# Eight PSUM banks for the transposed tiles of two norms, and the third norm's statistics split around the last residual additions

## The chip, the cores and the metric

The kernel runs on one core of a Trainium2 chip. The metric is the device time of one execution in microseconds (us); the median of three runs of the kernel before is 2484.04 us. A core has TensorE (PE, with its weight loads as PEld), VectorE (DVE), ScalarE (ACT), GpSimd (POOL) and SyncE (SP), which here only issues DMAs. PSUM, into which PE writes, has eight banks of 512 f32 columns over 128 partitions; the kernel names them `bank[:, 0..7, :]`.

## The reference, cut to what matters

One decoder layer on x of shape (2, 512, 512): two batches of 512 tokens with 512 features, so 1024 tokens in eight tiles of 128 (tiles 0 to 3 are the first batch, 4 to 7 the second). Three layer norms stand ahead of the causal attention, the group (self and cross) attention and the experts:

```python
x = x + attn(layernorm(x), ...)            # first norm, causal attention with 16 heads
x = x + xattn(layernorm(x), ctx_2048, ...) # second norm, 8 groups, self and cross attention, fp8 rounding
x = x + ffn(layernorm(x), ...)             # third norm, router, 8 experts with silu gate

def _layernorm(x, axis=-1, eps=1e-05):
    m = jnp.mean(x, axis=axis, keepdims=True)
    v = jnp.var(x, axis=axis, keepdims=True)
    return (x - m) / jnp.sqrt(v + eps)
```

## The kernel before, in words

The layer is written as blocks that follow each other: `first_norm`, `causal_attention`, `second_norm`, `group_attention`, `experts`. Each block holds one program for each engine, and all engines meet at its end before the next block begins; within a block only semaphores order them.

The residual stream is `X` in SBUF, eight tiles of 128 tokens x 512 f32. A norm has two halves.

**Statistics**, on DVE alone. `tile_stats` (L251) takes one `bn_stats` over a tile. `finish_stats` takes four `bn_aggr` (L259) and then a reciprocal square root in twelve tiny steps (L57 to L63), each waiting for the one before, and a shift (L263), which raises `s_shift`. It does so for the four tiles of a batch at once. `norm_stats` runs both over all eight tiles: four `bn_stats`, finish batch 0, four `bn_stats`, finish batch 1.

**Apply, turn, split**, in `norm_scalar` (ACT), `norm_tensor` (PE) and `norm_lo` (DVE). For each batch, ACT first writes four normalised tiles `xn` (L279), and then, for each of them, waits until PE has transposed it (four 128x128 f32 transposes into one bank, L293, `s_turned`) and copies the bank to the f16 high part `XTh` (L283, `s_hi`). DVE subtracts that from the bank, which gives the f16 low part `XTl` (L270, `s_lo`). ACT turns to the next batch's `xn` only behind the last `XTh` of this one. PE writes tile t into bank `t % 2`, and so before tile t it waits until the low part of tile t - 2 is done.

The first norm runs at the start of the kernel: `X` arrives by eight DMAs, then the weights of the first head quad. Its DVE program is `norm_stats`, then `w.split_lo` (L158, which needs the high part from POOL, L154), then `norm_lo`. The second norm (L1047, L1205) has code of its own and doesn't call the three functions; its statistics (after the causal attention) are already written as batch 0, additions, batch 1.

The third norm's statistics stand at the end of `group_attention`. There the last group's output is rounded to fp8 (`output_round` on DVE, `quantised` on POOL, L1485, into `cat`), PE runs four output jobs Y0 to Y3 for the second batch (eight matmuls each, L1781 and L1782, in two banks by turns, so that Y2 waits until Y0's sum has been added), and DVE adds each to `X` (`project_out`, L1657, semaphore `y_added`). `norm_stats` for `rows3` comes behind all four additions. The first batch's additions were done a step earlier.

`experts` begins with the third norm's apply, turn, split (`norm_scalar`, `norm_tensor`, `norm_lo`, on `eXTh` and `eXTl`). Beside it, SP issues the router's weights and the first expert's `raw_gate`, `raw_up`, `raw_down` (2 MB each). POOL writes the f16 high parts of gate and up (four pieces each, L1919), as they land. DVE goes on behind `norm_lo` with the router's low part `rwl` (L1978), and then the low parts of gate and up, four pieces each (`split_lo`, L1973). PE runs the router (96 small matmuls, behind `rwl` and the last low part), then the experts: for each of 16 blocks twelve gate matmuls and twelve up matmuls; the first gate matmul of an expert waits for all four low pieces of gate, the first up matmul for all four of up. From then on PE is never short of work for long.

The two functions that the changed lines call directly:

```python
def tile_stats(dve, n, src, t):
    dve.bn_stats(n.stats[:, t, :], src[:, t, :]).then_inc(n.s_stats, 1)
def finish_stats(dve, n, b, use=0):
    tiles = slice(BT * b, BT * (b + 1))
    for t in range(BT * b, BT * (b + 1)):
        dve.wait_ge(n.s_stats, NT * use + t + 1)
        dve.bn_aggr(n.mv[:, t, :], n.stats[:, t, :]).then_inc(n.s_mv, 1)
    dve.wait_ge(n.s_mv, NT * use + BT * (b + 1))
    rsqrt(dve, n.s_rsqrt, RSQRT_STEPS * (B * use + b), n.mv[:, tiles, 1], n.half[:, tiles], n.rstd[:, tiles],
          n.tmp[:, tiles])
```

Of the kernel before, what the change touches and what calls it, by code (L numbers as in the profile page):

```python
# [24 lines left out]
P = 128  # L25
# [3 lines left out]
BT = S // P  # L29
KT = D // P  # L30
# [16 lines left out]
def rsqrt(dve, sem, base, var, half, out, tmp):  # L47

    k = 0

    def step(ins):
        nonlocal k
        ins.then_inc(sem, 1)
        k += 1
        dve.wait_ge(sem, base + k)

    step(dve.tensor_scalar(half, var, EPS, None, ALU.add))  # L57
    step(dve.tensor_scalar(tmp.bitcast(I32), half.bitcast(I32), 1, None, ALU.arith_shift_right))
    step(dve.tensor_scalar(out.bitcast(I32), tmp.bitcast(I32), -1.0, RSQRT_SEED, ALU.mult, ALU.add))
    for _ in range(NEWTON):  # L60
        step(dve.tensor_tensor(tmp, out, out, ALU.mult))
        step(dve.scalar_tensor_tensor(out=tmp, in0=tmp, scalar=-0.5, in1=half, op0=ALU.mult, op1=ALU.mult))
        step(dve.scalar_tensor_tensor(out=out, in0=tmp, scalar=1.5, in1=out, op0=ALU.add, op1=ALU.mult))  # L63
    assert k == RSQRT_STEPS


def after(eng, sem, count):

    if not isinstance(count, int) or count > 0:
        eng.wait_ge(sem, count)  # L70
# [100 lines left out]
def first_norm(nc, ins, sem, sb, bank, X, ident, cols, XTh, XTl, x_d, w):  # L171
# [7 lines left out]
    with nc.Block() as block:  # L179
# [17 lines left out]
        @block.vector  # L197
        def _(dve):
            norm_stats(dve, rows, X, lambda t: dve.wait_ge(x_in[t], 16))
            w.split_lo(dve, 0)  # L200
            norm_lo(dve, tiles, XTh, XTl, bank)

        @block.scalar
        def _(act):
            norm_scalar(act, tiles, X, XTh, bank)

        @block.tensor
        def _(pe):
            pe.wait_ge(id_set, 2)
            norm_tensor(pe, tiles, bank, ident)  # L210
# [30 lines left out]
def norm_stats(dve, n, src, arrived, use=0):  # L241

    for t in range(NT):
        arrived(t)
        tile_stats(dve, n, src, t)
        if (t + 1) % BT == 0:
            finish_stats(dve, n, t // BT, use)
# [15 lines that stand above are left out]
    dve.scalar_tensor_tensor(out=n.shift[:, tiles], in0=n.mv[:, tiles, 0], scalar=-1.0, in1=n.rstd[:, tiles],  # L263
                             op0=ALU.mult, op1=ALU.mult).then_inc(n.s_shift, 1)


def norm_lo(dve, n, XTh, XTl, bank):
    for t in range(NT):
        dve.wait_ge(n.s_hi, t + 1)
        dve.tensor_tensor(XTl[:, :, t * P:(t + 1) * P], bank[:, t % 2, :].rearrange("p (k c) -> p k c", k=KT),  # L270
                          XTh[:, :, t * P:(t + 1) * P], ALU.subtract).then_inc(n.s_lo, 1)


def norm_scalar(act, n, X, XTh, bank):
    for b in range(B):
        tiles = range(BT * b, BT * (b + 1))
        act.wait_ge(n.s_shift, b + 1)
        for t in tiles:
            act.activation(n.xn[:, t, :], X[:, t, :], ACT.Identity, scale=n.rstd[:, t:t + 1],  # L279
                           bias=n.shift[:, t:t + 1]).then_inc(n.s_xn, 1)  # L280
        for t in tiles:
            act.wait_ge(n.s_turned, t + 1)
            act.activation(XTh[:, :, t * P:(t + 1) * P], bank[:, t % 2, :].rearrange("p (k c) -> p k c", k=KT),  # L283
                           ACT.Copy).then_inc(n.s_hi, 1)


def norm_tensor(pe, n, bank, ident):
    for t in range(NT):
        pe.wait_ge(n.s_xn, t + 1)
        if t >= 2:  # L290
            pe.wait_ge(n.s_lo, t - 1)
        for k in range(KT):
            ins = pe.transpose(bank[:, t % 2, k * P:(k + 1) * P], n.xn[:, t, k * P:(k + 1) * P], ident[:])  # L293
        ins.then_inc(n.s_turned, 1)


# [551 lines left out]
def round_fp8(dve, sem, base, y, unit, total):  # L848

    dve.tensor_scalar(y, y, FP8_MAX, -FP8_MAX, ALU.min, ALU.max).then_inc(sem, 1)
    dve.wait_ge(sem, base + 1)
    dve.tensor_scalar(unit.bitcast(U16), y.bitcast(U16), 0x7F80, 0x40, ALU.bitwise_and, ALU.bitwise_or).then_inc(sem, 1)
    dve.wait_ge(sem, base + 2)
    dve.tensor_scalar(unit, unit, 1.5 * 2.0 ** -6, 2.0 ** 4, ALU.max, ALU.mult).then_inc(sem, 1)
    dve.wait_ge(sem, base + 3)
    dve.tensor_tensor(total, y, unit, ALU.add).then_inc(sem, 1)
# [470 lines left out]
def group_attention(nc, ins, sem, sb, bank, X, ident, cols, rcols, xq, kv_d, gw, rows3, qr, v0):  # L1329
# [6 lines left out]
    STEPS = GROUPS * B  # L1336
# [29 lines left out]
    next_done, next_read, y_done, y_added = (sem(f"x_{x}") for x in ("next_done", "next_read", "y_done", "y_added"))  # L1366
# [39 lines left out]
    with nc.Block() as block:  # L1406
# [229 lines left out]
        def _(dve):  # L1636
# [17 lines left out]
            def project_out(n, t, b):  # L1654
                dve.wait_ge(y_done, y_count(t, n))
                x = X[:, BT * b + t, :]
                dve.scalar_tensor_tensor(out=x, in0=JOB[job_bank(f"Y{t}", n + 2)], scalar=psc[:], in1=x, op0=ALU.mult,  # L1657
                                         op1=ALU.add).then_inc(y_added, 1)
# [20 lines left out]
            def output_round(n, kind):  # L1679
                count = KINDS * n + kind  # L1680
                dve.wait_ge(o_read, count + 1)
                after(dve, rounded, count)
                round_fp8(dve, rounding, ROUND_STEPS * count, y[:], unit[:], total[:])
# [44 lines left out]
            parts_lo(STEPS - 1, UX - 1)  # L1728
            for kind in range(1, KINDS):
                output_round(STEPS - 1, kind)  # L1730
            for t in range(BT):
                project_out(STEPS - 1, t, 1)

            norm_stats(dve, rows3, X, lambda t: dve.wait_ge(y_added, BT * (STEPS - 1) + max(0, t - BT + 1)))

        @block.tensor
        def _(pe):
# [118 lines left out]
def experts(nc, ins, sem, sb, bank, X, ident, out_d, rows3):  # L1856
# [38 lines left out]
    with nc.Block() as block:  # L1895
# [39 lines left out]
        def _(act):  # L1935
            def split_hi(e, i, k):
# [3 lines left out]
                act.activation(piece(wh, i, k), piece(raw, i, k), ACT.Copy, scale=WS).then_inc(w_hi[i], 1)  # L1940

            norm_scalar(act, n, X, XTh, bank)
            act.wait_ge(rw_in, 16)
            act.activation(rwh[:], rw[:], ACT.Copy, scale=WS).then_inc(rw_hi, 1)
# [25 lines left out]
        def _(dve):  # L1970
            def split_lo(e, i, k):
                dve.wait_ge(w_hi[i], PW * e + k + 1)
                dve.scalar_tensor_tensor(out=piece(wl, i, k), in0=piece(raw, i, k), scalar=WS, in1=piece(wh, i, k),  # L1973
                                         op0=ALU.mult, op1=ALU.subtract).then_inc(w_lo[i], 1)

            norm_lo(dve, n, XTh, XTl, bank)
            dve.wait_ge(rw_hi, 1)
            dve.scalar_tensor_tensor(out=rwl[:], in0=rw[:], scalar=WS, in1=rwh[:], op0=ALU.mult, op1=ALU.subtract)\  # L1978
# [70 lines left out]
        @block.tensor  # L2049
        def _(pe):  # L2050
            norm_tensor(pe, n, bank, ident)
            pe.wait_ge(rw_lo, 1)
            pe.wait_ge(n.s_lo, NT)
# [98 lines left out]
```

## Time and profile before

| what | us |
|---|---|
| median of three runs (2480.91 to 2487.3) | 2484.04 |
| profiled execution, its own time | 2486.31 |
| its span, from the first to the last instruction | 2484.5 |
| PE busy | 2317.3 |
| DVE busy | 1415.6 |
| ACT busy | 1138.5 |
| POOL busy | 1152.1 |

The profiled execution's time is 1.8 us more than its span. Times in the profile count from the first instruction. The first norm lies at 0 to 28 us, the third norm's statistics at 1452 to 1463 us, its apply, turn and split at 1463 to 1477 us, and the experts from there to the end. "Granted clock" is the share of TensorE's full clock: 1.00 is 2.4 GHz and 0.50 is 1.2 GHz.

### The profile page before, as it was taken

What the parts mean: (1) busy time and instruction counts of PE and PEld (TensorE: products, weight loads), DVE (VectorE), ACT (ScalarE), POOL (GpSimd) and SP (SyncE); (2) the same over time, 40 slices, a digit from 0 to 9 for tenths busy, and PEclk for the clock granted to TensorE, in tenths of its full rate; (3) what the DMA queues carried; (4) which work ended last, traced back from release to release, by engine and by line L of the source; (5) the groups of instructions that cost most, each with busy time, mean ns of one, the idle gap of its engine ahead of it and who ended that gap; (6) DMA issues with size and microseconds to landing.
All of it is one profiled execution on the core that took longest, in us unless ns stands there. A gap on an engine that the chain in (4) does not pass through costs nothing. (4 is left out here: it accounts for less than half of the span.)

```text
span 2484.5 us, 39824 instructions
## 1 busy us (share of the span) xinstructions
PE 2317.3 (93%) x14528; PEld 1308.1 (53%) x14528; DVE 1415.6 (57%) x2936; ACT 1138.5 (46%) x2165; POOL 1152.1 (46%) x1396
## 2 busy tenths in 40 slices
PE   6899888968999999999999859999999999999999
PEld 3566544535666666666666534444444444444444
DVE  5766687437999989999999852222222222222221
ACT  3455465447777778877778721111111111111110
POOL 2422327656787878778786324131313131313131
PEclk9799799979999999999999969999999999999999
DMA  4100012127878888888888741101010101010000
GB/s 151 35 19 18 1 60 103 76 102 158 157 149 164 155 167 162 159 155 154 166 151 150 138 152 73 68 34 68 34 68 34 68 34 67 35 67 35 0 0 34
DMA packets 437986, 224.81 MB, mean 90 GB/s; under 512 B 406224, under 2 KB 410320, under 8 KB 433616
## 3 DMA queue, kind: packets, MB, share of 16 engines
q1 hardware_dynamic: 415952, 186.74, 33.0%
q10 hardware_dynamic: 21888, 36.19, 5.6%
q8 instruction: 84, 1.38, 0.2%
q14 instruction: 62, 0.51, 0.1%
HBM read 103.34 MB, written 18.87 MB: 49 GB/s over the span
## 5 line engine op out<-in xcount | busy, mean ns | idle before, releaser
L1955 ACT ACTIVATE sil<-bank 128x512 f32<-128x512 f32 x128 | 76.4, 597 | 772.4 <-PE bank L301 772.4
L1928 POOL TENSOR_SCALAR hh<-h 128x512 f16<-128x512 f32 x128 | 105.1, 821 | 679.4 <-DVE h L2026 679.4
L2026 DVE TENSOR_TENSOR h<-bank,sil 128x512 f32<-128x512 f32 x128 | 88.6, 692 | 530.6 <-PE bank L301 422.8
L1572 ACT ACTIVATE xprob<-bank,xnm 128x1024 f32<-128x1024 f32 (+1 forms) x240 | 220.2, 917 | 185.2 <-DVE xnm L1663 185.0
L1675 DVE SCALAR_TENSOR_TENSOR xparts<-xprob,xri,xparts 128x1024 f16<-128x1024 f32 (+1 forms) x240 | 273.2, 1138 | 3.3 <-ACT xparts L1580 3.2
L1663 DVE TENSOR_REDUCE xnm<-bank 128x1 f32<-128x512 f32 (+1 forms) x256 | 242.9, 949 | 50.7 <-PE bank L301 49.3
L1580 ACT ACTIVATE xparts<-xprob,xri 128x1024 f16<-128x1024 f32 (+1 forms) x240 | 227.7, 949 | 0.0
L299 PE MATMUL bank<-eXTh,ewh_gate 128*128 128x512 f16 x512 | 194.8, 380 | 3.5 <-DVE ewl_gate L1973 3.5
L300 PE MATMUL bank<-eXTh,ewl_gate 128*128 128x512 f16 x512 | 194.8, 380 | 0.0
L301 PE MATMUL bank<-eXTl,ewh_gate 128*128 128x512 f16 x512 | 194.7, 380 | 0.0
L299 PE MATMUL bank<-eXTh,ewh_up 128*128 128x512 f16 x512 | 194.1, 379 | 0.0
L300 PE MATMUL bank<-eXTh,ewl_up 128*128 128x512 f16 x512 | 194.0, 379 | 0.0
L301 PE MATMUL bank<-eXTl,ewh_up 128*128 128x512 f16 x512 | 194.0, 379 | 0.0
L299 PE MATMUL bank<-ewh_down,hh 128*128 128x512 f16 x512 | 194.0, 379 | 0.0
L300 PE MATMUL bank<-ewh_down,hl 128*128 128x512 f16 x512 | 194.0, 379 | 0.0
L301 PE MATMUL bank<-ewl_down,hh 128*128 128x512 f16 x512 | 194.0, 379 | 0.0
L2036 DVE SCALAR_TENSOR_TENSOR X<-bank,wcol,X 128x512 f32<-128x512 f32 x64 | 48.0, 751 | 214.9 <-PE bank L301 214.9
L1930 POOL TENSOR_TENSOR hl<-h,hh 128x512 f16<-128x512 f32 x128 | 153.3, 1198 | 22.6 <-POOL hh L1928 21.2
L299 PE MATMUL bank<-xpt,xkv 128*128 128x256 f16 x512 | 140.8, 275 | 8.9 <-DMA xpt<-xparts 8.8
L1470 POOL TENSOR_SCALAR qr<-qr,xrstd,xshift 128x128 f32<-128x128 f32 x240 | 147.4, 629 | 1.7
L300 PE MATMUL bank<-xpt,xkv 128*128 128x256 f16 x512 | 140.8, 275 | 0.0
L301 PE MATMUL bank<-xpt,xkv 128*128 128x256 f16 x512 | 140.7, 275 | 0.0
(289 smaller groups left out, 5966.7 us busy)
## 6 DMA issues: line engine op xcount, KB each, us to landing
xkv<-kv_made ACTq DMA_DIRECT2D x64, 256.0 KB, 3.3
raw_gate<-in_gate SPq DMA_DIRECT2D x8, 2048.0 KB, 7.8
raw_up<-in_up SPq DMA_DIRECT2D x8, 2048.0 KB, 7.9
raw_down<-in_down SPq DMA_DIRECT2D x8, 2048.0 KB, 7.8
xwraw<-in_w_group ACTq DMA_DIRECT2D x60, 256.0 KB, 3.4
kv_made<-vst SPq DMA_DIRECT2D x16, 512.0 KB, 4.2
kv_made<-kst SPq DMA_DIRECT2D x16, 512.0 KB, 2.6
kvraw<-in_w_kvx SPq DMA_DIRECT2D x4, 1024.0 KB, 6.7
```

The lines of the kernel that those rows point to most:

```text
L299: pe.matmul(ps, ah, bh, start=start, stop=False)
L300: pe.matmul(ps, al, bh, start=False, stop=False)
L301: return pe.matmul(ps, ah, bl, start=False, stop=stop)
L1470: pool.tensor_scalar(norm_block(i), norm_block(i), rstd[:, i:i + 1], shift[:, i:i + 1], ALU.mult, ALU.add)\
L1572: act.activation(prob[prob_of(u)][:, 0:L], SC[u % 2][:, 0:L], ACT.Exp, bias=nm[:, u % 4:u % 4 + 1], accum_out=rs[:, u % 4:u % 4 + 1]).then ...
L1580: act.activation(parts[u % PARTS_KEPT][:, 0:L], prob[prob_of(u)][:, 0:L], ACT.Copy, scale=ri[:, u % 4:u % 4 + 1]).then_inc(hi, 1)
L1663: dve.tensor_reduce(nm[:, s:s + 1], SC[u % 2][:, 0:L], AX.X, ALU.max, negate=True).then_inc(maxed, 1)
L1675: dve.scalar_tensor_tensor(out=part[:, L:2 * L], in0=prob[prob_of(u)][:, 0:L], scalar=ri[:, u % 4:u % 4 + 1], in1=part[:, 0:L], op0=ALU.mu ...
L1928: pool.tensor_scalar(hh[half][:, f, :], h[i % 2][:], 1.0, 1.0, ALU.mult, ALU.mult).then_inc(h_hi, 1)
L1930: pool.tensor_tensor(hl[half][:, f, :], h[i % 2][:], hh[half][:, f, :], ALU.subtract).then_inc(h_lo, 1)
L1955: act.activation(sil[i % 2][:], bank[:, 2 * (i % 2), :], ACT.Silu, scale=1.0 / WS).then_inc(silu, 1)
L2026: dve.tensor_tensor(h[i % 2][:], bank[:, 2 * (i % 2) + 1, :], sil[i % 2][:], ALU.mult).then_inc(made, 1)
```

## The change

In the first and the third norm, tile t is transposed into bank t instead of bank `t % 2`, and PE's wait for the low part of tile t - 2 is gone. At the end of `group_attention`, the first batch's third-norm statistics are issued on DVE ahead of the last four `project_out`, and only the second batch's behind them; the waits on `y_added` are placed accordingly.

```diff
 def norm_lo(dve, n, XTh, XTl, bank):
     for t in range(NT):
         dve.wait_ge(n.s_hi, t + 1)
-        dve.tensor_tensor(XTl[:, :, t * P:(t + 1) * P], bank[:, t % 2, :].rearrange("p (k c) -> p k c", k=KT),
+        dve.tensor_tensor(XTl[:, :, t * P:(t + 1) * P], bank[:, t, :].rearrange("p (k c) -> p k c", k=KT),
                           XTh[:, :, t * P:(t + 1) * P], ALU.subtract).then_inc(n.s_lo, 1)
...
         for t in tiles:
             act.wait_ge(n.s_turned, t + 1)
-            act.activation(XTh[:, :, t * P:(t + 1) * P], bank[:, t % 2, :].rearrange("p (k c) -> p k c", k=KT),
+            act.activation(XTh[:, :, t * P:(t + 1) * P], bank[:, t, :].rearrange("p (k c) -> p k c", k=KT),
                            ACT.Copy).then_inc(n.s_hi, 1)
 
 
 def norm_tensor(pe, n, bank, ident):
     for t in range(NT):
         pe.wait_ge(n.s_xn, t + 1)
-        if t >= 2:
-            pe.wait_ge(n.s_lo, t - 1)
         for k in range(KT):
-            ins = pe.transpose(bank[:, t % 2, k * P:(k + 1) * P], n.xn[:, t, k * P:(k + 1) * P], ident[:])
+            ins = pe.transpose(bank[:, t, k * P:(k + 1) * P], n.xn[:, t, k * P:(k + 1) * P], ident[:])
         ins.then_inc(n.s_turned, 1)
...
             for kind in range(1, KINDS):
                 output_round(STEPS - 1, kind)
+            dve.wait_ge(y_added, BT * (STEPS - 1))
+            for t in range(BT):
+                tile_stats(dve, rows3, X, t)
+            finish_stats(dve, rows3, 0)
             for t in range(BT):
                 project_out(STEPS - 1, t, 1)
-
-            norm_stats(dve, rows3, X, lambda t: dve.wait_ge(y_added, BT * (STEPS - 1) + max(0, t - BT + 1)))
+            for t in range(BT):
+                dve.wait_ge(y_added, BT * (STEPS - 1) + t + 1)
+                tile_stats(dve, rows3, X, BT + t)
+            finish_stats(dve, rows3, 1)
```

## Rows read from the trace of the kernel before

**Rows 1.** The page: busy time of each engine, and the chain that ended last, by line.
```profile
PE 2317.3 (93%) x14528; PEld 1308.1 (53%) x14528; DVE 1415.6 (57%) x2936; ACT 1138.5 (46%) x2165; POOL 1152.1 (46%) x1396
...
PE bank L299 13%; PE bank L300 13%; PE bank L301 13%; DVE ewl_gate L1973 0%; ACT xn_n L279 0%; PE bank L293 0%; ACT eXTh L283 0%; DVE eXTl L270 0%; DVE rwl L1978 0%; DVE X L2036 0%
```

**Rows 2.** The chain in order of time, third norm: start, us, what.
```profile
1463.06 2.93 ACT xn_n L279 x4
...
1476.68 0.69 DVE eXTl L270
1477.38 0.96 DVE rwl L1978
1478.33 6.23 DVE ewl_gate L1973 x4
```

**Rows 3.** Timeline, first norm: start, us, engine, line, operation [idle before, releaser].
```profile
10.23 2.93 ACT L279 ACTIVATE xn_n<-X,shift_n,rstd_n 128x512 f32<-128x512 f32 x4 [8.22 <-DVE shift_n L263]
...
11.19 1.94 PE L293 MATMUL bank<-ident,xn_n 128*128 128x128 f32 x8 [11.19 <-ACT xn_n L279]
...
13.07 1.06 ACT L283 ACTIVATE XTh<-bank 128x512 f16<-128x512 f32 x2
...
15.28 0.16 DVE L263 SCALAR_TENSOR_TENSOR shift_n<-mv_n,rstd_n 128x4 f32<-128x4 f32 x1
15.36 1.75 DVE L158 SCALAR_TENSOR_TENSOR wl<-wraw,wh 128x1536 f16<-128x1536 f32 x1
17.03 1.28 DVE L270 TENSOR_TENSOR XTl<-bank,XTh 128x512 f16<-128x512 f32 x2
...
17.86 1.94 PE L293 MATMUL bank<-ident,xn_n 128*128 128x128 f32 x8 [4.73 <-DVE XTl L270]
18.98 0.60 ACT L283 ACTIVATE XTh<-bank 128x512 f16<-128x512 f32 x1 [4.86 <-PE bank L293]
...
20.33 2.92 ACT L279 ACTIVATE xn_n<-X,shift_n,rstd_n 128x512 f32<-128x512 f32 x4
...
27.20 0.69 DVE L270 TENSOR_TENSOR XTl<-bank,XTh 128x512 f16<-128x512 f32 x1 [0.16 <-ACT XTh L283]
28.18 0.20 POOL L406 MEMSET identb<- 128x128 bf16 x1 [15.32 <-POOLq L179]
```

**Rows 4.** Timeline, end of the group attention, 1440 to 1458 us.
```profile
1440.45 1.15 POOL L1485 TENSOR_TENSOR cat<-xtotal,xunit 128x512 f16<-128x512 bf16 x1 [5.40 <-DVE xtotal L858]
...
1445.36 0.75 DVE L1657 SCALAR_TENSOR_TENSOR X<-bank,psc,X 128x512 f32<-128x512 f32 x1 [4.98 <-PE bank L1782]
...
1447.89 0.38 PE L1781 MATMUL bank<-xw3h,cat 128*128 128x512 f16 x1
...
1451.54 0.75 DVE L1657 SCALAR_TENSOR_TENSOR X<-bank,psc,X 128x512 f32<-128x512 f32 x1 [0.98 <-PE bank L1782]
1452.21 2.46 DVE L251 BATCH_NORM_STATS2 stats_n<-X 128x6 f32<-128x512 f32 x4
...
1457.45 2.46 DVE L251 BATCH_NORM_STATS2 stats_n<-X 128x6 f32<-128x512 f32 x4
```

**Rows 5.** Timeline, DVE, statistics of the second norm, near 307 us.
```profile
306.83 1.15 DVE L57 TENSOR_SCALAR half_n<-mv_n 128x4 f32<-128x4 f32 x1
```

**Rows 6.** Timeline, POOL, DVE and PE, first expert's weights; x1 rows are single pieces.
```profile
1471.34 4.07 POOL L1919 TENSOR_SCALAR ewh_gate<-raw_gate 128x1024 f16<-128x1024 f32 x4 [29.73 <-DMA raw_gate<-in_gate]
1476.24 6.11 POOL L1919 TENSOR_SCALAR ewh_up<-raw_up 128x1024 f16<-128x1024 f32 x4 [0.83 <-DMA raw_up<-in_up]
...
1479.39 2.05 DVE L1973 SCALAR_TENSOR_TENSOR ewl_gate<-raw_gate,ewh_gate 128x1024 f16<-128x1024 f32 x1
...
1484.48 4.62 DVE L1973 SCALAR_TENSOR_TENSOR ewl_up<-raw_up,ewh_up 128x1024 f16<-128x1024 f32 x4
...
1489.15 0.39 PE L299 MATMUL bank<-eXTh,ewh_up 128*128 128x512 f16 x1
```

**Rows 7.** Windows: busy us (instructions) of each engine, granted clock, DMA share, GB/s.
```profile
60.00:65.00 5.00, 5.00 (x43) 3.05 (x42) 2.76 (x6) 2.63 (x9) 5.00 (x11) 0.50 0.00 1
```

## The prediction

> **What bounds the kernel now.** I read the page's busy times and its chain first. PE is busy for 2317.3 us of 2484.5, and the chain that ended last consists of PE's matmuls but for a few small links of the third norm [rows 1]. So in most of the kernel an idle engine costs nothing, and only a stretch in which PE has no work can be shortened by this change. The busy share doesn't find such stretches; the chain in order of time and the timeline do. There are three:
>
> - 10 to 28 us. Nothing of the causal attention can begin before the first norm's block ends. The last instruction of that block is DVE's eighth low part at 27.20 us, and the next block's first instruction follows at 28.18 [rows 3].
> - 1452 to 1463 us. PE is out of work, and DVE takes the statistics of both batches, one behind the other [rows 4].
> - 1463 to 1489 us. The chain runs through the third norm's ACT, PE and DVE links, then the router's low part, then the four low pieces of gate [rows 2]; the low pieces of up end at 1484.48 + 4.62 = 1489.10, and the first up matmul starts at 1489.15 [rows 6]. What sets the experts' pace is therefore the end of up's low pieces, not the end of the norm.
>
> What comes behind each of these is relative to the block's start or to that up matmul, so a us taken off the last event of a stretch is a us off the end.
>
> **First norm, banks.** PE's wait before tile 2 is for tile 0's low part. DVE gives it only at about 17.7 us, since its batch-1 statistics (to 15.44) and the weight split of 1.75 us stand ahead of it. So PE idles 4.73 us, ACT waits 4.86 us for tile 2, and ACT's second batch starts at 20.33, though its shift was ready at 15.44 [rows 3]. Without the wait:
>
> - PE: eight transposes take 1.94 us with the last one's 0.42 in it, so they start 0.217 apart and a tile is 0.87. The tiles start at 11.19, 12.06, 12.93 and 13.80.
> - ACT: a high part started 18.98 - 17.86 = 1.12 us behind its tile's first transpose. Tile 2's starts at 14.05 and tile 3's at 14.92. ACT is free at 15.4, and the second batch's `xn` starts at about 15.5 instead of 20.33.
> - From `xn` to the first high part took 13.07 - 10.23 = 2.84, and to the first transpose 0.96. High parts 4 and 5 start at 18.3 and 18.8. The tiles 6 and 7 start at 18.2 and 19.1, their high parts at 19.3 and 20.2, and the last is done at 20.8.
> - DVE: it begins its low parts at 17.03 as now; two take 1.28, so a step is 0.60. Eight steps without a wait put the last start at 17.03 + 7 x 0.60 = 21.23, behind ACT's 20.8. So DVE is late last, not ACT or PE.
>
> The block's last instruction starts at 21.23 instead of 27.20: **-5.97 us**. Should each low part wait for a semaphore and take the whole 0.69 of a single one, it is 17.03 + 7 x 0.69 = 21.86, or -5.3. A faster PE clock would change nothing, as DVE sets the end. I take 5.97, since the pairs show 0.60. The weight DMA and POOL's split end before 15.36, as L158 needs them, and SP has nothing after them but the small `cols` load, so nothing else holds this block.
>
> **Third norm, statistics.** One batch takes 1457.45 - 1452.21 = 5.24 us on DVE [rows 4]. The first batch's moves ahead of the additions, into a hole: DVE finished its rounding just before POOL's `cat` at 1440.45 and idled 4.98 us until 1445.36 [rows 4]. Started at 1440.4, it ends at 1445.6, so the first addition is late by 0.3 us. What is queued behind it is Y0's addition, and Y2 on PE waits for that. Y2 starts at 1447.89 today, while the addition would end at 1445.6 + 0.75 = 1446.4. So there are 1.5 us of slack, and the chain Y0 to Y3 and the last addition at 1451.54 don't move. The second batch follows at 1452.21 as the first does now and ends 5.24 us sooner: **-5.24 us** for the block's end. The new waits on `y_added` hold nothing: the first batch's additions are a step old, and each of the second batch's is issued at least three `bn_stats` or additions ahead of the wait for it.
>
> Two neighbours need a price. `cat` runs beside the moved `bn_stats` and releases PE's Y0. If `bn_stats` held it up for its whole length, it would be at most 1.15 us, all of it on the path. In the first norm POOL's split ran beside four `bn_stats` and was in time for L158, and ACT's and DVE's rows there show no delay, so I take 0. The other is DVE's own L57. In the second norm's statistics, which already have this form, it took 1.15 us instead of 0.17 beside a POOL `tensor_tensor` [rows 5]. Here `cat` ends at 1441.6 and L57 comes at about 1440.4 + 2.4 + 0.4 = 1443.2, so they don't meet; if they did, 1.0 us would still fit in the 1.5 of slack. Cost 0.
>
> The Trainium skill says the same of such a pair: "SBUF — State Buffer", section "Who interferes with whom", lets a DVE `tensor_scalar` in a two-port mode take a port that it shares with GpSimd and wait for GpSimd's whole instruction. By that rule alone the move could cost DVE up to one `cat`; the sum would stay the same by it, because of the slack.
>
> **Third norm, banks.** Count from ACT's first `xn`, at 1463.06 [rows 2]. Today the last low part starts at 13.62 there. By the steps above: tile 3 starts at 0.96 + 2.61 = 3.57, its high part at 4.69, the second `xn` at 5.15, tile 7 at 8.72, its high part at 9.84, and its low part at 10.5. That is 3.1 us sooner, and it would be the whole gain if DVE could go on at the same pace. It can't. DVE's next work, `rwl` and eight low pieces, has two SBUF inputs, and POOL's high pieces run at the same time. A high piece alone takes 4.07 / 4 = 1.02 us, but the four of up take 6.11; a low piece alone takes 4.62 / 4 = 1.15, but 2.05 where POOL is at work, and `rwl`, a 128x32 tile, needs 0.96 [rows 2, 6]. They take turns. From 1478.33 to 1489.10 the pair did eight low pieces and two of up's high pieces in 10.8 us, so a high piece in turn adds 10.8 - 8 x 1.14 = 1.7 for two, or 0.84 each.
>
> POOL's pieces don't move: gate's data land at 1471.34 and up's at 1476.24, 8.28 and 13.18 by this count [rows 6]. DVE comes to `rwl` at 11.1, in the third of gate's high pieces, and gets its turn at 11.3. Then every turn is taken: eight low pieces at 1.14, and five high pieces (gate's last and all four of up, where today only two are left) at 0.84. 11.3 + 0.1 + 9.1 + 4.2 = 24.7, against 26.04 today. So up's low pieces end **1.3 us** sooner, and I take 1.2, as the other order (POOL's last gate piece first, at 1.0) gives 1.1. The low bound is POOL's and DVE's whole work back to back from 8.28: 8 x 1.02 + 0.1 + 8 x 1.14 = 17.4, or 25.7 against 26.04: 0.4. The high bound is 3.1.
>
> Gate's matmuls start some 2 to 3 us sooner, at 18.4 to 19.6, but they wait for up's weights again afterwards: twelve of them at half clock (0.43 each) take 5.1 us and end before 24.7. So that start is worth nothing, and the stall moves from ahead of gate to between gate and up.
>
> **Sum.** 5.97 + 5.24 + 1.2 = 12.4 us. From the profiled execution's own time, 2486.31, that gives 2473.9 (the 1.8 us around the span stay). It was 2.3 us over the median of the runs; against 2484.04 the time is **2471.6 us**, 0.50% less.
>
> **Rivals.**
>
> - *The whole 3.1 us of the third norm come through,* since POOL, waiting, falls behind without holding DVE. For it: `rwl` and the next low piece ran in one go. Against it: single low pieces at 2.05 [rows 6]. 14.3 us, 2469.7. Chance 0.1.
> - *The first norm's gain does not reach the end,* because the causal attention's start is held by something that doesn't move with the block. All I see there is relative (1 us from the block's start at 28.18). Then 6.4 us are left, 2477.6, which is within 0.3% (7.5 us; that is about what a measurement of this kernel tells from no change). Chance 0.07.
> - *The clock falls in the new gap between gate and up,* so that up's first matmuls run at 1.2 GHz. Some eight of them at 0.43 instead of 0.22 is 1.7 us; the gap is about 1 us. 10.7 us, 2473.3. This is inside the first case's range. Chance 0.12.
> - *Slower: the causal attention runs longer at half clock.* There PE is full and yet the granted clock is 0.50 at times, as at 60 to 65 us [rows 7]. Starting 6 us earlier could shift those stretches. Each us more of full PE work at half clock costs 0.5 us. To end 7.5 us above today it needs 20 us of loss, or 40 us more of half clock; half of that, 10 us of loss, leaves 2.4 us and ends within 0.3%. For it: nothing in the kernel holds the clock up there. Against it: the three runs differ by 6.4 us in all. At the price of 40 us it gives 2491.6. Chance 0.04 for slower, 0.07 for the milder case.
>
> My own case has 0.6.
>
> **How the numbers follow.** Faster by over 0.3%: the sum's case, the whole 3.1 us and the clock gap, 0.82. Within 0.3%: the first norm's loss and the milder clock case, 0.14. Slower: 0.04. The likeliest case alone has 11.0 (5.3 + 5.2 + 0.4) to 14.3 us of gain, widened by the runs' spread of 3 us either way: 2467 to 2476. The range of 8 in 10 takes in the first norm's loss on the upper side and the full third-norm gain with the spread on the lower: 2466 to 2479.
>
> **What would show it.** In the first norm: PE's eight tiles in two bursts of four, `xn` of the second batch near 15.5, the last low part near 21.2, and the next block near 22.2. At the group attention's end: `bn_stats` beside `cat`, the first addition about 0.3 us later against `cat`, Y2 not later, and 5.2 us from the last addition to the end of the statistics instead of 10.5. In the experts, counted from the first `xn`: the last low part near 10.5, more than one low piece at 2 us, gate near 19, PE idle before up, and the first up matmul near 24.8. It is wrong if the low pieces keep 1.15 us beside POOL, if Y0 starts later against the rounding, or if the stretch between the first norm and the third changes its length by more than about 3 us.

## The result and the profile after

The changed kernel took 2474.79 us (median of six runs), the kernel before 2485.28 (six runs, its first three among them); the ratio is 0.9953, with a 95% interval of 0.9936 to 0.9970. That is 10.5 us by the medians, where 12.4 were forecast, and the time lies in the range, 3.2 us above the 2471.6 that were forecast. The interval of the ratio stands for 7 to 16 us, so the whole time alone can't tell 12.4 from 10.5; the stretches of the profile can. In a later run of the changed kernel two of eleven executions took 13443 and 10487 us at a granted clock of 1.00, for a cause that no run shows; they are left out of its figures below. The profiled execution has a span of 2473.5 us against 2484.5, so 11.0 us less.

The chain that ended last, in order of time, for the changed kernel (start, us, what):

```profile
1453.43 0.82 ACT xn_n L279
1454.30 3.69 PE bank L291 x16
1458.01 0.60 ACT eXTh L283
1458.60 2.81 ACT xn_n L279 x4
1461.42 0.49 ACT eXTh L283
1461.93 2.48 DVE eXTl L270 x4
1464.41 0.27 DVE rwl L1982
1464.69 7.97 DVE ewl_gate L1977 x4
1472.66 5.39 DVE ewl_up L1977 x4
1478.10 0.39 PE bank L297
```

Against [rows 2], the third norm is shorter, gate's low pieces are longer (7.97 against 6.23), and up's low pieces are now a link of the chain: PE waits for them, not only for gate's. The first norm in the timeline of the changed kernel:

```profile
10.72 3.65 PE L291 MATMUL bank<-ident,xn_n 128*128 128x128 f32 x16 [10.72 <-ACT xn_n L279]
11.80 1.48 POOL L154 TENSOR_SCALAR wh<-wraw 128x1536 f16<-128x1536 f32 x1 [10.32 <-DMA wraw<-in_w_qkv]
...
12.42 0.88 DVE L57 TENSOR_SCALAR half_n<-mv_n 128x4 f32<-128x4 f32 x1
...
15.71 2.93 ACT L279 ACTIVATE xn_n<-X,shift_n,rstd_n 128x512 f32<-128x512 f32 x4 [0.71 <-DVE shift_n L263]
...
16.57 3.33 PE L291 MATMUL bank<-ident,xn_n 128*128 128x128 f32 x16 [2.21 <-ACT xn_n L279]
17.26 4.86 DVE L270 TENSOR_TENSOR XTl<-bank,XTh 128x512 f16<-128x512 f32 x8
18.55 2.02 ACT L283 ACTIVATE XTh<-bank 128x512 f16<-128x512 f32 x4
22.41 0.20 POOL L404 MEMSET identb<- 128x128 bf16 x1 [9.13 <-POOLq L179]
```

PE works in two bursts of sixteen transposes, the second `xn` starts at 15.71 instead of 20.33 [rows 3], and DVE runs its eight low parts without one wait: 4.86 us for eight, of which a single one takes 0.69, so (4.86 - 0.69) / 7 = 0.60 a step. The group attention's end in the timeline of the changed kernel:

```profile
1435.94 2.47 DVE L251 BATCH_NORM_STATS2 stats_n<-X 128x6 f32<-128x512 f32 x4
1436.10 1.15 POOL L1483 TENSOR_TENSOR cat<-xtotal,xunit 128x512 f16<-128x512 bf16 x1 [5.39 <-DVE xtotal L856]
1437.40 0.58 PE L1785 MATMUL bank<-xw3h,cat 128*128 128x512 f16 x1 [3.54 <-POOL cat L1483]
...
1438.71 0.17 DVE L57 TENSOR_SCALAR half_n<-mv_n 128x4 f32<-128x4 f32 x1
...
1441.18 0.75 DVE L1655 SCALAR_TENSOR_TENSOR X<-bank,psc,X 128x512 f32<-128x512 f32 x1
...
1447.14 0.75 DVE L1655 SCALAR_TENSOR_TENSOR X<-bank,psc,X 128x512 f32<-128x512 f32 x1 [0.98 <-PE bank L1786]
1447.81 2.46 DVE L251 BATCH_NORM_STATS2 stats_n<-X 128x6 f32<-128x512 f32 x4
```

`cat` takes 1.15 us beside the moved `bn_stats`, as in [rows 4], L57 keeps its 0.17, and the first addition comes 5.08 us behind `cat` instead of 4.91. Cut at events that both timelines have, the two spans compare like this:

| stretch | before | after | difference | forecast |
|---|---|---|---|---|
| start to the next block's first instruction | 28.18 | 22.41 | -5.77 | -5.97 |
| to the first matmul of Y0 (not touched) | 1413.57 | 1414.99 | +1.42 | 0 |
| to the first `bn_stats` behind the last addition | 10.46 | 10.41 | -0.05 | 0 |
| to the experts' first `xn` | 10.85 | 5.62 | -5.23 | -5.24 |
| to the first up matmul | 26.09 | 24.67 | -1.42 | -1.2 |
| to the end | 995.35 | 995.40 | +0.05 | 0 |
| sum | 2484.5 | 2473.5 | -11.0 | -12.4 |

So the three stretches of the change gave 12.4 us together, and the 1.4 that are missing went in the long stretch between them that it doesn't touch.

### The profile page after: what moved, and what is told of

Its sections match the earlier page's. It is cut to its first block and busy times, and to the rows that moved or that the text cites. A ratio compares the mean times of both kernels' runs of the same rounds, so it can differ in the third digit from the quotient of the medians.

```text
span 2473.5 us, 39812 instructions
## 1 busy us (share of the span) xinstructions
PE 2314.8 (94%) x14528; PEld 1308.3 (53%) x14528; DVE 1421.5 (57%) x2936; ACT 1137.8 (46%) x2165; POOL 1150.5 (47%) x1396
```

## The experiments

Each kernel has a profile and 5 to 11 timed executions. The kernel before was timed beside each of them, and its median stands behind "against"; only the ratio to it compares kernels of different groups. The numbers in brackets are the ratio's 95% interval. "Next block", "statistics" and "up" are the first, fourth and fifth stretch of the table, in the kernel's own profile. For one kernel each of these is a single profile. All kernels compute the whole layer.

**One part each.** The first norm's banks alone, the third norm's banks alone, the statistics alone. The edit for the first, against the changed kernel (cut; the comment is added, and ACT's and PE's calls get the same 2):

```diff
-            dve.wait_ge(y_added, BT * (STEPS - 1))
-            for t in range(BT):
-                tile_stats(dve, rows3, X, t)
...
+            norm_stats(dve, rows3, X, lambda t: dve.wait_ge(y_added, BT * (STEPS - 1) + max(0, t - BT + 1)))
...
-            norm_lo(dve, n, XTh, XTl, bank)
+            norm_lo(dve, n, XTh, XTl, bank, 2)   # third norm: two banks and the wait, as before
```

> Only the first norm has eight banks; the third norm keeps two, and its statistics stay behind the additions. My theory: the block of the first norm ends 5.8 us sooner (next block at 22.4 instead of 28.18 from the start of the span), all of it reaches the end, and the third norm's stretches stay as before (10.8 us of statistics, 26.1 us from the first xn to the first up matmul). Time ratio about 0.9977. Rival (the gain is lost in the causal attention): the stretch from the end of the first norm to the second norm's start grows from 291.8 us by about 6.

Measured: 2480.66 us against 2485.83, ratio 0.9981 (0.9963 to 0.9999); next block at 22.62, statistics 10.86, up 26.00. The theory holds: 5.6 us in that stretch. The causal attention took 287.0 us in this profile, against 291.8, so it did not grow. One profile would not show that by itself, as this length varies by up to 9 us between profiles of the same code (see below). But it is 281.4 to 291.7 us in the eleven profiles with the banks in the first norm, and 286.5 to 291.9 in the three without, so the rival's 6 us more are not there.

> Only the third norm has eight banks. My theory (DVE and POOL take turns): the last low part comes 3 us sooner, but the first up matmul comes 24.7 us behind the first xn instead of 26.1, a gain of 1.4; ratio 0.9994. Rival (the whole 3.1 us arrive): up at 23.0. First norm as before, next block near 28.2.

Measured: 2485.06 us against 2485.83, ratio 0.9995 (0.9977 to 1.0012); up at 24.56, so 1.5 us sooner than before, although the last low part is done at 10.98 instead of 14.31, 3.3 us sooner. The rival with all 3.1 us falls. The whole time can't show a gain of this size.

> Only the third norm's statistics are changed. My theory: from the second batch's first bn_stats to the experts' first xn 5.6 us instead of 10.85, so 5.2 us of gain; the output jobs Y0 to Y3 take 9.8 us from the first matmul to the last addition's start, as before; ratio 0.9979. Rival (bn_stats beside cat delays Y0, or the later first addition delays Y2): the stretch from cat to the last addition grows by about 1 us, and the gain is 4.

Measured: 2481.6 us against 2485.83, ratio 0.9972 (0.9951 to 0.9994); statistics 5.62, and Y0 to the last addition's start 9.93 us against 9.79. The rival falls. Up came at 27.21 here, 1.1 later than before, with two banks in both. Up's low pieces ended 0.7 later, at 26.72: up's data landed 0.9 us later in this execution (POOL's first up piece at 14.04 behind the first `xn` instead of 13.18), so that POOL's pieces fell further into DVE's. The other 0.4 is PE itself: its gate matmuls began 0.7 later too, at 22.24, at a spacing of 0.43 us, and the first up matmul followed them without a gap, 0.5 behind the low pieces. So the low pieces set the pace only where they end behind the gate matmuls.

**The changed kernel once more.**

> The changed kernel once more, for a second profile of it and for the spread. The three stretches of the change should repeat within 0.3 us (next block near 22.4, statistics 5.6, first xn to up 24.7). The stretches between them, which the change leaves alone, should differ by 1 to 5 us from the first profile of this kernel if the 1.4 us that they lost there come from the clock, and repeat within 0.3 us if the change itself caused the loss. Ratio 0.9953.

Measured: 2473.75 us (nine executions) against 2485.83, ratio 0.9952 (0.9931 to 0.9972); next block at 22.36, statistics 5.62, up 24.76. The three stretches repeat within 0.1 us. The untouched stretch took 1418.7 us, 3.7 more than in the first profile of the same kernel, so a difference of this size doesn't need a change of the kernel.

**Who takes the third norm's other 2 us.** The high pieces of up on ACT, which has nothing to do there:

```diff
-            for i in range(2):
+            for i in range(1):
                 wait(raw_in[i], 16)          # POOL: high pieces of gate only
...
+            for k in range(PW):              # ACT, behind the router's high part
+                act.wait_ge(raw_in[1], 16)
+                act.activation(piece(wh, 1, k), piece(raw, 1, k), ACT.Copy, scale=WS).then_inc(w_hi[1], 1)
```

> The changed kernel, with the four high pieces of the first expert's up weights on ACT (idle there) instead of POOL. My theory (the low pieces lose their time to turns with POOL): POOL's only overlap is gate's last pieces, the low pieces take 1.15 us each, up's end near 21 us behind the first xn instead of 24.7, and the up matmuls then wait for PE's own gate matmuls: first up matmul at 21 to 22, 3 us of gain over the changed kernel. Rival (the landing of up's data, 13.1, sets the end): up at 24 or later, no gain.

Measured: 2470.04 us against 2483.29, ratio 0.9944 (0.9927 to 0.9961); up at 21.91, 2.8 us sooner than in the changed kernel. The data can't be what set the end. The up matmuls did not wait for PE's own gate matmuls, as I had expected, but for up's low pieces, which end at 21.85, 0.9 later than expected. The DVE timeline of this kernel shows that one turn of POOL was left, and another in front of `rwl`:

```profile
1459.82 1.03 DVE L1985 SCALAR_TENSOR_TENSOR rwl<-rw,rwh 128x32 f16<-128x32 f32 x1
1460.77 5.45 DVE L1980 SCALAR_TENSOR_TENSOR ewl_gate<-raw_gate,ewh_gate 128x1024 f16<-128x1024 f32 x4
1466.15 4.62 DVE L1980 SCALAR_TENSOR_TENSOR ewl_up<-raw_up,ewh_up 128x1024 f16<-128x1024 f32 x4
```

Up's four pieces take 4.62 us, 1.15 each, while gate's take 5.45: one of them waited 0.8 for POOL's last gate piece.

> As the kernel with up's high pieces on ACT, but the third norm with two banks as before. If the turns with POOL were what swallowed half of the banks' gain, up's low pieces end 3 us later here than with eight banks (near 23.7 behind the first xn), the whole 3.1 us of the banks. If something else swallowed it, the difference is again 1.4 us.

Measured: 2472.59 us against 2483.29, ratio 0.9953 (0.9936 to 0.9970). Up's low pieces end at 23.49, only 1.6 us later than with eight banks. My expectation of 3 was wrong: gate's pieces on POOL were still in play. With two banks DVE comes to `rwl` when POOL is done with them (`rwl` 0.18 us, gate 4.62), with eight it comes earlier and pays twice, 0.85 in front of `rwl` and 0.83 in gate. 3.3 - 0.85 - 0.83 = 1.6. So POOL had to go altogether:

```diff
-            for i in range(2):               # POOL: no high pieces
-                wait(raw_in[i], 16)
...
+            for i in range(2):               # ACT: gate, then up
+                act.wait_ge(raw_in[i], 16)
+                for k in range(PW):
+                    act.activation(piece(wh, i, k), piece(raw, i, k), ACT.Copy, scale=WS).then_inc(w_hi[i], 1)
```

> The changed kernel, with the high pieces of the first expert's gate and up both on ACT, behind the router's high part; POOL has no work beside DVE's low pieces. My theory: every low piece takes 1.15 us, except that gate's follow ACT's high pieces (0.97 each from 10.4 behind the first xn): gate's matmuls start near 15.6, up's low pieces end near 20.3, and the first up matmul waits for PE's gate matmuls, near 20.7 (21.9 with gate on POOL, 24.7 in the changed kernel). Rival (DVE isn't held by POOL, the pieces are slow for another reason): low pieces of 2 us remain.

Measured: 2468.99 us against 2487.66, ratio 0.9936 (0.9914 to 0.9959); gate at 15.80, up's low pieces end at 20.29, up at 20.34. In the DVE timeline of this kernel every link is at its own pace:

```profile
1458.86 0.18 DVE L1980 SCALAR_TENSOR_TENSOR rwl<-rw,rwh 128x32 f16<-128x32 f32 x1
1459.07 4.63 DVE L1975 SCALAR_TENSOR_TENSOR ewl_gate<-raw_gate,ewh_gate 128x1024 f16<-128x1024 f32 x4
1463.62 4.63 DVE L1975 SCALAR_TENSOR_TENSOR ewl_up<-raw_up,ewh_up 128x1024 f16<-128x1024 f32 x4
```

> The same without POOL, and the third norm with two banks. The turns are gone altogether, so the whole 3.3 us that the eight banks take off the last low part should now arrive at the end of up's low pieces: near 23.4 against 20.3, a difference of 3.0 (it was 1.4 with both on POOL and 1.6 with gate alone on POOL). Rival (something else swallows it): again near 1.5.

Measured: 2473.96 us against 2487.66, ratio 0.9946 (0.9928 to 0.9964); up's low pieces end at 23.86, 3.6 us later than with eight banks. That is the whole 3.3 us of the last low part, and 0.3 of a wait for ACT's first gate piece. So the banks' gain, read at the end of up's low pieces, is whole where POOL is silent, 1.6 with gate's pieces on POOL, and 1.3 and 1.5 with both (two pairs of profiles whose data landed alike: the first norm's banks alone against the changed kernel, and the kernel before against the third norm's banks alone). In the two kernels with two banks and high pieces on ACT the first up matmul (23.83 and 24.09) followed PE's own gate matmuls without a gap, 0.2 to 0.3 behind the low pieces.

**What sets the end of the first norm.** The first quad's low weight part moved from DVE to POOL:

```diff
             w.split_hi(pool)
+            pool.wait_ge(w.hi, 1)
+            pool.tensor_scalar(w.raw[:], w.raw[:], WS, 1.0, ALU.mult, ALU.mult).then_inc(id_set, 1)
+            pool.wait_ge(id_set, 3)
+            pool.tensor_tensor(w.l[:], w.raw[:], w.h[:], ALU.subtract).then_inc(w.lo, 1)
...
-            w.split_lo(dve, 0)
```

> The changed kernel, with the first quad's low part of the weights computed on POOL instead of DVE. My theory (DVE sets the end of the first norm, ACT comes 0.6 to 1.2 us behind it): the next block starts 1.0 us sooner, near 21.4, as ACT's last high part near 20 us holds DVE's last low part then. Rival (ACT or PE already set the end): no gain, 22.4. POOL needs about 1.5 + 1.5 + 3.5 us from 11.8 on and is done by 18.5; its pieces may hold one of DVE's tiny statistics steps for up to 3.5 us, which would cost the whole gain and more.

Measured: 2473.81 us against 2483.29, ratio 0.9966 (0.9950 to 0.9982); next block at 25.89, 3.5 us later than in the changed kernel. The side risk came true. In the timeline of this kernel two statistics steps of four columns last until POOL's instruction ends, 1.16 and 2.77 us longer than their 0.17:

```profile
13.01 1.47 POOL L197 TENSOR_SCALAR wraw<-wraw 128x1536 f32<-128x1536 f32 x1
13.17 1.33 DVE L57 TENSOR_SCALAR half_n<-mv_n 128x4 f32<-128x4 f32 x1
...
14.56 3.09 POOL L199 TENSOR_TENSOR wl<-wraw,wh 128x1536 f16<-128x1536 f32 x1
14.74 2.94 DVE L59 TENSOR_SCALAR rstd_n<-tmp_n 128x4 int32<-128x4 int32 x1
```

> Both edits together. If they add, next block near 21.4 and up at 21 to 22 us behind the first xn: 4 us faster than the changed kernel, ratio to before about 0.9937.

Measured: 2470.68 us against 2483.29, ratio 0.9953 (0.9932 to 0.9974); next block at 25.62 and up at 21.44. The second edit adds its part, the first costs as it does alone. So the first was repeated with one more wait, `pool.wait_ge(rows.s_shift, 2)`, ahead of POOL's new work:

> The changed kernel, with the first quad's low weight part on POOL, but only behind the second batch's shift, so that it meets none of DVE's tiny statistics steps (beside them it made one of them take 2.94 us instead of 0.17, and the next block came at 25.9). L59 back at 0.17; DVE's low parts start near 15.6, the last waits for ACT's last high part near 20.1, and the next block comes near 21.7 against 22.4. Rival (POOL's 4.6 us from 15.5 on now set the end, or the tensor_tensor on POOL holds DVE's low parts): 22.4 or later.

Measured: 2471.27 us against 2487.66, ratio 0.9946 (0.9926 to 0.9967); next block at 21.69, as expected. The timeline of this kernel, where DVE now waits for ACT:

```profile
17.09 3.11 POOL L200 TENSOR_TENSOR wl<-wraw,wh 128x1536 f16<-128x1536 f32 x1
18.32 2.17 ACT L287 ACTIVATE XTh<-bank 128x512 f16<-128x512 f32 x4
18.93 2.48 DVE L274 TENSOR_TENSOR XTl<-bank,XTh 128x512 f16<-128x512 f32 x4 [1.08 <-ACT XTh L287]
21.69 0.20 POOL L408 MEMSET identb<- 128x128 bf16 x1 [1.50 <-POOLq L179]
```

So in the changed kernel DVE did set that end, but with ACT close behind it. How close is read best from ACT's first `xn` to the next block, less what POOL's instructions added to the statistics steps. That is 17.93 to 17.95 us in the three profiles with two banks in the first norm, 11.93 to 11.94 in the seven with eight banks and the low weight part on DVE, and 11.45 here (21.69 - 10.24) and in the kernel with POOL's early work (25.89 - 10.51 - 1.16 - 2.77). So the weight part off DVE is worth 0.5 us; the 0.7 between 22.41 and 21.69 are these 0.5, 0.7 that L57 waited in the changed kernel and not here, and 0.5 the other way, by which the first `xn` came sooner there. DVE's low parts, which read one operand from PSUM, keep their 0.60 a step beside POOL's `tensor_tensor`.

**Both edits that helped, together.**

> Both: no high pieces on POOL at the experts' start, and the low weight part on POOL behind the shift. Next block near 21.7, up near 20.7 behind the first xn: 4.7 us faster than the changed kernel, ratio to before near 0.9935.

Measured: 2464.87 us against 2487.66, ratio 0.9917 (0.9888 to 0.9946), the lowest here. Up at 20.24, 4.4 us sooner than in the changed kernel. The next block came at 22.31, 0.1 sooner than in the changed kernel. The edit did its part: from the first `xn`, at 10.54 here and at 9.76 there, and less L57's wait of 0.3 for POOL's high part (L154, 12.19 to 13.66), it is 11.45 us again. What hid it is that the first `xn` itself was 0.8 late in this execution. In the whole time its interval still overlaps that of the changed kernel (0.9936 to 0.9970); that it is faster is shown by the stretches alone.

## Why the prediction was right

**First norm, -5.97 forecast, -5.77 measured.** The step "DVE is late last" holds, and so does the 0.60 a step. The 0.2 are L57: it took 0.88 us beside POOL's L154 (11.80 to 13.28), where it was clear of it before. I had priced this very collision for the third norm from [rows 5] and not looked for it in the first, where the landing of `X` and of the weights decides it. The first batch's `xn` came 0.47 sooner, and L57 lasted 0.71 longer. Without the two the gain is 5.77 - 0.47 + 0.71 = 6.0, and the seven profiles above agree (17.94 - 11.94).

**Statistics, -5.24 forecast, -5.23 measured.** Both prices of 0 hold: `cat` 1.15, L57 0.17, Y0 to the last addition unchanged. The first addition was late by 0.17 us, and Y2 didn't notice. The second profile and every kernel with this part show 5.61 to 5.63.

**Third norm, banks, -1.2 forecast, -1.42 measured.** The last low part was done 3.3 us sooner, and the low pieces then took turns with POOL's high pieces. Single pieces in the changed kernel's timeline:

```profile
1464.61 2.12 DVE L1977 SCALAR_TENSOR_TENSOR ewl_gate<-raw_gate,ewh_gate 128x1024 f16<-128x1024 f32 x1
1466.65 2.05 DVE L1977 SCALAR_TENSOR_TENSOR ewl_gate<-raw_gate,ewh_gate 128x1024 f16<-128x1024 f32 x1
1468.63 2.05 DVE L1977 SCALAR_TENSOR_TENSOR ewl_gate<-raw_gate,ewh_gate 128x1024 f16<-128x1024 f32 x1
1470.61 2.05 DVE L1977 SCALAR_TENSOR_TENSOR ewl_gate<-raw_gate,ewh_gate 128x1024 f16<-128x1024 f32 x1
1471.56 2.01 POOL L1923 TENSOR_SCALAR ewh_up<-raw_up 128x1024 f16<-128x1024 f32 x1
1472.58 2.05 DVE L1977 SCALAR_TENSOR_TENSOR ewl_up<-raw_up,ewh_up 128x1024 f16<-128x1024 f32 x1
...
1478.10 0.39 PE L297 MATMUL bank<-eXTh,ewh_up 128*128 128x512 f16 x1 [0.56 <-DVE ewl_up L1977]
```

Five low pieces of some 2 us stand here; the kernel before has two, one of them in [rows 6]. The last line is the first up matmul, which waited for them. The Trainium skill's "SBUF — State Buffer", section "Who interferes with whom", has the rule behind both this and L57's wait: a DVE instruction with two SBUF inputs contends with a GpSimd instruction that reads SBUF, a `tensor_scalar` in a two-port mode does too, and the second to issue blocks for the first's whole length. The runs agree (2.05 against 1.15 for a low piece; 2.94 against 0.17 for L59 beside POOL's early work); that L57 and L59 ran in a two-port mode is inferred from their waits, no run shows the mode.

**Gate's matmuls, "worth nothing".** They started at 19.28 instead of 21.55, and PE then waited 0.56 us for up's low pieces. The clock didn't fall in that gap: up's matmuls run 0.22 apart. That rival falls for this profile.

**The sum.** The three stretches gave 12.4 us, as forecast, but that they do so to 0.0 is luck: 0.2 too much in the first norm and 0.2 too little in the third cancel. Of the 3.2 us between the forecast time and the measured one, 1.2 is the median of the kernel before, which moved from 2484.04 to 2485.28 with three more executions; the other 1.9 is the gain in the whole time, 10.5 instead of 12.4.

**The term that was off: 0 for the untouched stretch.** It was 1.4 us longer in this profile. The causal attention (next block to the second norm's first `xn`) was 0.7 shorter, 291.1 against 291.8; what follows it, up to Y0, was 2.1 longer, 1123.9 against 1121.7. So the rival of a longer causal attention did not happen in this pair. What such differences are worth is seen in six profiles of kernels whose code is the same up to the experts: the changed kernel, its second run, and the four with high pieces of the first expert on ACT and the first norm as in the changed kernel. Their causal attention took 291.1, 291.7, 286.8, 291.6, 282.2 and 291.3 us, what follows it 1123.9, 1127.0, 1123.8, 1125.1, 1128.4 and 1124.8, and the whole untouched stretch 1415.0, 1418.7, 1410.6, 1416.8, 1410.6 and 1416.1. The kernel before and the one with the third norm's banks alone are the same code up to there, too, and differ by 2.5 (1413.6 and 1411.1). The windows over the causal attention and over its last 51 us, for the changed kernel:

```profile
22.41:313.53 291.12, 263.19 (x2496) 165.51 (x2497) 197.41 (x437) 139.49 (x417) 98.27 (x104) 0.86 0.11 38
...
262.41:313.53 51.12, 39.25 (x283) 22.41 (x282) 33.69 (x96) 17.43 (x53) 15.45 (x9) 0.60 0.00 1
```

and, for the one without POOL at the experts' start, over all of it and over its last 42 us:

```profile
22.24:304.48 282.24, 253.30 (x2496) 161.12 (x2497) 196.40 (x437) 138.93 (x417) 98.39 (x104) 0.91 0.11 39
262.24:304.48 42.24, 29.41 (x289) 18.21 (x288) 34.10 (x98) 17.65 (x56) 15.45 (x9) 0.86 0.00 1
```

The same 2496 matmuls, PE busy for 253.3 us at a mean granted clock of 0.91 or for 263.2 at 0.86. In the first 240 us the two executions are level (2214 and 2209 matmuls); all of the 8.9 us lies in the last piece, with a granted clock of 0.86 in one and 0.60 in the other. So a loss of this kind belongs to the execution and comes with the clock, and it needs no change of the kernel. The rival of a longer causal attention had the right place and the right size of price, up to 9 us, but it strikes either kernel alike. What decides in which way an execution falls is open; no run here was made to tell it.

For the 1.4 us themselves no cause is shown. They are well inside what the same code does (8 us), but no run shows either that the change costs nothing there: the 1121.7 of the kernel before is the lowest of fourteen values. For the same reason one of the prediction's signs of being wrong, a stretch that changes by more than 3 us, could not tell anything: the second profile of the changed kernel has 5.1 us more there than the kernel before. And the gap of 2 us between the forecast gain and the medians has no cause that these runs could show.

## What to carry to other kernels

Cut the span at events that both kernels have and compare stretch by stretch: two pairs of profiles gave 1.3 and 1.5 us for one term, while whole times of one kernel spread over 7 us and more. Count from an event that the change doesn't move, such as the first `xn`, not from the start of the span: that is how a gain of 0.5 us showed itself in three profiles, one of which seemed to have next to none, and one a loss. Extra buffers speed up a pipeline only until its next shared resource: before crediting a norm that ends 3 us sooner, look at what the engine does next, and at who runs beside it. Where DVE and POOL both read SBUF, move POOL's share to an idle ACT, or out of the way of DVE's chain of tiny steps; a step of 0.17 us can cost 2.9.

## What the runs showed that I had not expected

- The causal attention's length comes in steps. Over fourteen profiles it lies near 291.5 (six), near 286.8 (five, 286.2 to 287.7) or near 282 (three, 281.4 to 282.4), some 4.7 us apart. In the last piece before the second norm the kernel before has a granted clock of 0.65 over 51.8 us, and the one without POOL 0.86 over 42.2.
- The order in which POOL and DVE take turns isn't fixed. In some executions POOL's gate pieces took 5.13 us and up's 7.93, in others 4.08 and 7.08, and in the five profiles with eight banks and both on POOL up's low pieces ended at 24.5 to 24.9 behind the first `xn` all the same.
